# The first routing group computed inside the attention drain, in a transformer block with a mixture of experts

## The reference, cut to what matters

```
x = x + attn_a(layernorm(x))
x = x + ffn(layernorm(x))
x = x + attn_b(layernorm(x))
x = x + ffn(layernorm(x))

def ffn(flat):                                   # 2048 rows
    logits = flat @ router_w                     # 64 experts
    scores = softmax(logits)
    idx    = top_k(logits + router_bias, 4)
    gate   = scores[idx] / scores[idx].sum()
    routed = sum over the 4 of gate * ((silu(flat@wg[e]) * (flat@wu[e])) @ wd[e])
    shared = (silu(flat @ swg) * (flat @ swu)) @ swd
    return routed + shared
```

## Time and profile before

| what | us |
|---|---|
| median of three runs | 1123.34 (1122.24 to 1132.47) |
| the profiled execution's own time | 1131.23 |
| span from its first to its last instruction | 1129.6 |
| PE busy in it | 892.8 (79%) |
| DVE busy | 709.6 (63%) |
| POOL busy | 495.2 (44%) |
| ACT busy | 460.4 (41%) |
| mean granted clock of PE, as a share of full speed | 0.889 |

### The profile page before, as it was taken

The page is one execution under the profiler, slowest core; times in us unless marked ns, Lnnn a source line. Parts: engine busy times, 40 slices in busy tenths (PEclk is TensorE's granted clock), DMA queues, the critical chain, the costliest instruction groups (busy, mean ns, idle before and its releaser), DMA issues. The chain is left out here.

```text
span 1129.6 us, 23684 instructions
## 1 busy us (share of the span) xinstructions
PE 892.8 (79%) x7450; PEld 674.7 (60%) x7450; DVE 709.6 (63%) x2262; ACT 460.4 (41%) x974; POOL 495.2 (44%) x575
## 2 busy tenths in 40 slices
PE   6986999989898888992755799998999797998000
PEld 5764666658787766881644445547888576786000
DVE  6877888846987333553555789946887543454333
ACT  3643565552110444663334468872111144564000
POOL 3000344331777432325772234428577532331775
PEclk9986899998999899996786799998999899999555
DMA  7483999909995799863496677605824498974443
GB/s 263 91 162 66 188 249 235 277 11 267 236 247 163 233 274 271 260 205 115 131 191 169 112 107 114 90 1 130 202 98 136 154 276 249 272 244 144 126 130 116
DMA packets 159162, 197.86 MB, mean 175 GB/s; under 512 B 17376, under 2 KB 137696, under 8 KB 155872
## 3 DMA queue, kind: packets, MB, share of 16 engines
q1 hardware_dynamic: 105920, 101.96, 40.9%
q0 software_dynamic: 22848, 68.18, 18.9%
q10 hardware_dynamic: 30272, 26.22, 7.9%
HBM read 132.86 MB, written 90.18 MB: 197 GB/s over the span
## 5 line engine op out<-in xcount | busy, mean ns | idle before, releaser
L893 ACT ACTIVATE tmp<-ps 128x256 f32<-128x256 f32 (+1 forms) x344 | 155.7, 478 | 115.3 <-PE ps L846 40.6
L518 POOL DMA_INDIRECT xd<-big,slot x128 | 130.2, 1017 | 71.7 <-issue 37.8
L1013 ACT ACTIVATE tmp<-ps 128x384 f32<-128x384 f32 (+1 forms) x256 | 134.9, 544 | 63.5 <-PE ps L662 37.5
L557 POOL DMA_INDIRECT big<-yd,slot x128 | 125.1, 977 | 42.7 <-issue 26.8
L472 POOL COPY arena<-negmax 24x2048 bf16<-24x2048 bf16 x32 | 60.5, 1892 | 136.1 <-ACT negmax L893 91.0
L1152 DVE SCALAR_TENSOR_TENSOR X<-big,comb,X 128x256 f32<-128x256 f32 x128 | 60.1, 483 | 90.7 <-DMA big<-yd,slot 90.5
L579 PE MATMUL ps<-arena 96*128 96x256 bf16 (+1 forms) x512 | 98.8, 280 | 17.2 <-DVE tmp L1203 6.9
L1545 DVE SCALAR_TENSOR_TENSOR tmp<-tmp,ps 128x128 f32<-128x128 f32 x128 | 36.8, 288 | 107.0 <-ACT tmp L1080 106.5
L659 PE MATMUL ps<-arena 120*128 120x256 bf16 (+1 forms) x512 | 101.3, 265 | 0.6 <-ACT tmp L1013 0.2
L1555 DVE COPY tmp<-ps 128x256 f32<-128x256 f32 x128 | 53.8, 424 | 59.0 <-PE ps L875 40.0
L608 PE MATMUL ps<-xt,weights 128*128 128x256 f32 x256 | 72.8, 447 | 22.8 <-ACT xt L893 22.5
(11 more groups left out here) (185 smaller groups left out, 1834.3 us busy)
## 6 DMA issues: line engine op xcount, KB each, us to landing
big<-xd POOLq DMA_DIRECT2D x128, 256.0 KB, 4.7
arena<-parts SPq DMA_DIRECT2D x192, 128.0 KB, 6.0
xd<-zero SPq DMA_DIRECT2D x8, 2048.0 KB, 14.4
spill<-in_we SPq DMA_DIRECT2D x128, 128.0 KB, 2.8
yd<-tmp POOLq DMA_DIRECT2D x64, 256.0 KB, 3.2
yd<-tmp ACTq DMA_DIRECT2D x64, 256.0 KB, 3.3
arena<-in_we SPq DMA_DIRECT2D x8, 1024.0 KB, 8.6
yd<-zero SPq DMA_DIRECT2D x8, 1024.0 KB, 24.6
```

The lines of the kernel that those rows point to most:

```text
L518: pool.indirect_dma_start(xd[:, :], bass.IndirectOffsetOnAxis(ap=slot[:, i, k:k + 1], axis=0), xn_all[:, i, :], None).then_inc(scattered.s ...
L557: pool.indirect_dma_start(gring[n % GRING], None, yd[:, :], bass.IndirectOffsetOnAxis(ap=slot[:, b * TB + m % TB, m // TB:m // TB + 1], ax ...
L893: return act.activation(dst, src, ACT.Copy)
L1013: act.activation(prob[h % 8][:, 0:n], ps[2 + h % 2][:, 0:n], ACT.Exp).then_inc(exp_ready.sem, 1)
```

## The change

Round 0: `turn_normal(0)`, `turn_normal(1)` and `logits(0)` go into the attention's step s = B (behind heads 0 and 3), with DVE's `pick(0)` behind its `group` of head 4; `ranks(0)` and `place(0)` go to step s = B+1. The turned tiles use other PSUM banks there. Round 1: the two turns go into the projection loop behind batches 4 and 5, `logits(0)` behind the loop, `ranks(0)` behind `shared_in(0, 0)`, and DVE does `pick(0)` and `place(0)` one after the other ahead of its first `shared_gate`. In both rounds `pick` and `place` of the other groups each come one shared batch earlier on DVE, `ranks(3)` moves from step 4 to step 3, `share_tiles` moves ahead of `shared_gate(5)`, and the turns and logits of the next group follow `shared_in(s, 1)`. In round 0 POOL scatters two tiles before it normalises the last batch. `EARLY` equals B, so no shared batch moves. The scratch tiles of the routing lie in `spill` now. The diff, cut:

```diff
         def turn_bank(r, b):
+            return ps[7] if b >= TB else ps[b if r == 0 else 2 + b]
+        def rank_bank(r, g):
+            return ps[6] if g else ps[1 if r == 0 else 4]
 # POOL
-                for b in range(B - 1 if r == 0 else 0, B):
-                    normal_rows(b)
+                if r == 1:
+                    for b in range(B):
+                        normal_rows(b)
...
                 for i in range(NT):
+                    if r == 0 and i == TB:
+                        normal_rows(B - 1)
                     if i % 4 == 0:
                         pool.wait_ge(*slot_ready(r, i // 4 + 1))
 # PE, attention loop
+                        if s == B and h == 0 and r == 0:
+                            pe.wait_ge(*mx_ready(r, B * H))
+                            turn_normal(0)
+                            turn_normal(1)
+                        if s == B and h == 3 and r == 0:
+                            logits(0)
+                        if s == B + 1 and h == 3 and r == 0:
+                            ranks(0)
 # PE, projection loop of round 1
+                        if b in (4, 5):
+                            turn_normal(b - 4)
+                    logits(0)
 # PE, shared_in
+                    if s == 0 and half == 1:
+                        pe.wait_ge(*rank_out(r, 1))
 # PE, routing stage
-                turn_normal(0)
-                turn_normal(1)
-                logits(0)
-                turn_normal(2)
-                turn_normal(3)
-                for s in range(B + 1):
-                    if s < B:
+                for s in range(EARLY + 1):
+                    if s < EARLY:
                         shared_in(s, 0)
+                    if s == 0 and r == 1:
+                        ranks(0)
                     if s >= 1:
                         shared_out(s - 1)
-                    if s in (1, 2):
+                    if s < EARLY:
+                        shared_in(s, 1)
+                    if s in (0, 1, 2):
                         turn_normal(2 * s + 2)
                         turn_normal(2 * s + 3)
-                    if s < B:
-                        shared_in(s, 1)
-                    if s in (0, 1, 2, 4):
-                        ranks(min(s, 3))
-                    if s < 3:
                         logits(s + 1)
+                    if s in (1, 2, 3):
+                        ranks(s)
                     if s == 5:
                         pe.wait_ge(*tef_ready(r, 1))
                         pe.transpose(ps[6][0:1, 3 * P:4 * P], tef, ident[:, :]).then_inc(teT_done.sem, 1)
 # ACT, attention loop and projection loop
+                        if s == B and h in (0, 1) and r == 0:
+                            keep_turned(h)
+                        if b in (5, 6):
+                            keep_turned(b - 5)
 # ACT, routing stage
-                for b in range(4):
-                    keep_turned(b)
                 exponents(0)
-                for s in range(B):
+                for s in range(EARLY):
                     shared_tanh(s, 0)
-                    if s in (1, 2):
+                    if s in (1, 2, 3):
+                        exponents(s)
+                    shared_tanh(s, 1)
+                    if s in (0, 1, 2):
                         keep_turned(2 * s + 2)
                         keep_turned(2 * s + 3)
-                    if s in (1, 2, 4):
-                        exponents(min(s, 3))
-                    shared_tanh(s, 1)
 # DVE, attention loop
+                        if s == B and h == 4 and r == 0:
+                            clear_ranks()
+                            pick(0)
+                        if s == B + 1 and h == 4 and r == 0:
+                            place(0)
 # DVE, routing stage
-                pick(0)
+                if r == 1:
+                    clear_ranks()
+                    pick(0)
+                    place(0)
                 shared_gate(0)
-                place(0)
                 pick(1)
                 shared_gate(1)
-                dve.wait_ge(*rp_ready(r, NT))
                 add_shared(0)
                 place(1)
                 pick(2)
                 shared_gate(2)
                 add_shared(1)
                 place(2)
+                pick(3)
                 shared_gate(3)
                 add_shared(2)
-                pick(3)
+                place(3)
+                name_tiles()
                 shared_gate(4)
                 add_shared(3)
-                place(3)
-                name_tiles()
-                shared_gate(5)
-                add_shared(4)
                 share_tiles()
                 gates(0)
                 gates(1)
-                shared_gate(6)
-                add_shared(5)
+                shared_gate(5)
+                add_shared(4)
                 gates(2)
                 gates(3)
                 gates(4)
```

More of the change, by code:

```diff
@@ L50 @@
 EMPTY = E + 128 * E
+EARLY = B
 class Signal:
@@ L1331, in add_out @@
                     variance(r, b)
-                for s in range(B + 2):
-                    first, second, third = s < B, 1 <= s <= B, s >= 2
-                    for h in range(H):
-                        if first:
-                            if s * H + h >= early_maxima:
-                                maximum(s, h)
-                            if h % 8 == 7:
-                                split_maxima(s, h // 8)
-                        if third and h == 0:
-                            group(s - 2, 2)
-                        if third and h == 4:
-                            group(s - 2, 3)
-                        if second and h in (8, 12):
-                            group(s - 1, h // 4 - 2)
-                        if third and h == 9 and r == 0:
-                            dve.wait_ge(op_done.sem, s - 1)
-                            add_out(s - 1, x_added, ps[7])
@@ L1451, in place @@
                     dve.wait_ge(*slot_ready(r, g + 1))
+                for s in range(B + 2):
+                    first, second, third = s < B, 1 <= s <= B, s >= 2
+                    for h in range(H):
+                        if first:
+                            if s * H + h >= early_maxima:
+                                maximum(s, h)
+                            if h % 8 == 7:
+                                split_maxima(s, h // 8)
+                        if third and h == 0:
+                            group(s - 2, 2)
+                        if third and h == 4:
+                            group(s - 2, 3)
+                        if s == B and h == 4 and r == 0:
[3 more added lines that the diff above has]
+                            place(0)
+                        if second and h in (8, 12):
+                            group(s - 1, h // 4 - 2)
+                        if third and h == 9 and r == 0:
+                            dve.wait_ge(op_done.sem, s - 1)
+                            add_out(s - 1, x_added, ps[7])
+                if r == 1:
+                    dve.wait_ge(bias_added.sem, B)
+                    for b in range(B + 1):
+                        if b < B:
+                            dve.wait_ge(op1_done.sem, b + 1)
+                            xb = X[:, b * TB:b * TB + TB, :]
+                            dve.tensor_tensor(xb, xb, ps[6 + b % 2][:, :].rearrange("p (t d) -> p t d", t=TB), ALU.add).then_inc(x1_added.sem, 1)
+                        if b >= 1:
+                            dve.wait_ge(x1_added.sem, b)
+                            for i in range((b - 1) * TB, b * TB):
+                                dve.bn_stats(stats[:, i, :], X[:, i, :]).then_inc(stat_a.sem, 1)
+                            variance(r, b - 1)
                 def name_tiles():
@@ L1532, in _ @@
                 gates(4)
-                shared_gate(7)
-                add_shared(6)
+                for s in range(6, EARLY):
+                    shared_gate(s)
+                    add_shared(s - 1)
                 gates(5)
@@ L1537, in _ @@
                 gates(7)
-                add_shared(7)
+                add_shared(EARLY - 1)
                 barrier(dve, "dve")
```

158 lines of the change are left out of this document (76 added, 82 removed).

## The result

| kernel | median us | runs | range |
|---|---|---|---|
| before | 1127.9 | 4 | 1122.24 to 1137.21 |
| changed | 1147.68 | 4 | 1142.11 to 1152.7 |

The ratio is 1.0193, with a 95% interval of 1.0143 to 1.0243: the change costs 19.8 us between the medians, 1.9%. The profiled execution of the changed kernel took 1152.7 us (span 1151.1, mean clock 0.884 against 0.889), 21.5 more than the one of before. Each is above its median, by 5.0 and 3.3 us, so the traces tell where the time goes and the medians how much it is.

The account below looks back on a forecast made before the run. POOL's scatter chain and the PE-DVE shared-expert chain were taken to bound the kernel together. Round 0 +2.1, round 1 +9.0 and clock +6 made 17, taken as 16: 1123.3 + 16 = 1139 us, range 1133 to 1146.

Parts of the forecast that it names:

- Scatter chain: POOL's scatters up to the first expert load: 11.6 us earlier in round 0, 4.5 in round 1, if nothing else were late.
- Head start of 6.8 and drain: Round 0, attention's end: the drain grows 2.9 us, yet PE begins `shared_in(0, 0)` at 255.0 instead of 261.79.
- Stall at pick(3): PE at step 3, both rounds: waits for DVE, 4.2 us at `ranks(3)` and 0.9 at `shared_in(4, 0)`, 5.1 together.
- The 1.4 at step 5: PE at `shared_in(5, 0)`: waits 1.4 us for DVE's `place(3)` and `name_tiles`, absorbing clock loss from step 4's stalls.
- Stall at share_tiles: PE at `shared_in(6, 0)`: waits for DVE's `share_tiles`, two gates and half a gate, 6.1 us in round 0, 6.2 in round 1.
- Round 1: Start of round 1's shared experts: PE stalls 3.8 us in `ranks(0)` behind `pick(0)`, then 1.6 behind `place(0)`.
- The clock: Slower PE clock behind five idle stretches of 3.8 us or more, two in round 0, three in round 1: +6 us, between 0 and 14.
- The stalls and moves without the clock: Both rounds' routing up to the experts: +2.1 us in round 0 and +9.0 in round 1, +11.1 in sum.
- The rest of the program: Outside the altered stages nothing else that moves costs time; the expert stages keep their length.
- 11 + 14 = 25: Dearer rival: every PE stall drops the clock, for as long as 7 us; total 1148 us, chance 0.10.
- the faster ones: Rival: the scatter was the bound and PE and DVE had slack, so 11.6 and 4.5 us are kept; 1107 us, chance 0.11.
- It decides at `share_tiles`: Faster rival's test: PE keeps its head start only without waits there and at `pick(3)`; without the `share_tiles` stall, sum near +1.

Follow-up runs that it names:

- e9: The kernel before, unaltered, run and traced once more on another chip; ratio 0.9988 to the kernel before.
- e13: The changed kernel with `share_tiles` and its gates back behind `shared_gate(5)` and `add_shared(4)`; ratio 1.0049 to the kernel before.
- e15: The kernel before with only group 0's move, in both rounds, and the changed POOL order; ratio 0.9879 to the kernel before.
- e16: The kernel before with only `share_tiles`, `gates(0)` and `gates(1)` moved ahead of `shared_gate(5)` and `add_shared(4)`; ratio 1.0141 to the kernel before.

## Why the prediction was right in direction and short in size

I forecast +16 and got +19.8; 1139 lies 8.7 below the median, 4.6 of which is that the kernel before itself measured 1127.9 with a fourth run.

- **Scatter chain:** right in round 0: 257.7, 289.9 and 355 forecast, 258.51, 289.79 and 354.85 found. In round 1, counted from its attention, the first scatter came as forecast (794.4; found 804.96 with the attention's end 10.1 later), but POOL then waited 6.71 for group 1 where I had 3.9, and the first load came 2.7 earlier, not 4.5. It was rightly called useless behind PE's stalls.
- **Head start of 6.8 and drain:** right; PE began at 254.08, 255.0 forecast. The drain cost 3.8 where I had 2.9. In the kernel before, that place ran at the lower clock (rows 3 show 3.62 and 3.63 us for eight products that take 1.99 elsewhere); I read the times but gave nothing for this going away.
- **Stall at pick(3):** I had 4.2 + 0.9 = 5.1; it was 3.34 + 0.32 and 3.13 + 0.46. The 1.4 at step 5 didn't come. DVE took what I gave it (16.2 us from the second half of gate 2, at 297.36, to gate 3 at 313.52, against 16.4); it was PE that came later, through the slow products that begin at 278.73 (3.4 us of clock).
- **Stall at share_tiles:** 6.1 and 6.2 forecast, 6.15 and 6.16 found, with 7.83 idle ahead of it on DVE where I had 9.
- **Round 1:** 3.8 and 1.6 forecast at `ranks(0)`, 3.81 and 1.45 found.
- **The clock: this is the step that failed.** The term of +6 was mis-sized: between the two traces it was 11.2, and 17.4 against e9. I priced five stalls at 1.7 (three) and 0.5 (two) us, 6.1 in all; they cost 3.1, 3.1, 2.1, 1.5 and 2.3, 12.1 in all. The wait of 1.4 at step 5 that was to absorb part of it didn't come. I also left out that the clock falls behind the packed turns at step 1 (278.73 in round 0, 821.24 and 824.79 in round 1), with no stall over 1 us ahead: 6.8 more. And the wait of 2.82, behind which I had read nearly full rate, was followed by 5.29 us for products that take 3.62 (1.5 more). On the other side stand the 9.2 us of lower clock that the kernel before had in its trace. What makes the clock fall behind the packed turns in eight rounds of ten and not in the other two stays open.
- The stalls and moves without the clock: 11.1 forecast; 13.5 found in the drain and the two stages (3.8 + 20.9 - 11.2), 13.8 against e9. This part held, within 3 us.
- The rest of the program, which I had said would keep its length: 1.7 us longer between the stages, 4.9 shorter behind the second. In e9 the last part is as short (232.8 against the changed kernel's 232.4), so this is the spread between executions. By it the sum of the traces, 21.5, came nearer to my 17 than the terms did: that much is luck.

The Trainium skill ("TensorE: Matmul & The Clock Gate", HAM oscillation) has TensorE start slow again behind each of a row of waits for a DMA, and I noted that by it the sum would come near the upper end, 11 + 14 = 25. This case's trace agrees for the waits: all five were followed by slow products, 12.1 us of a possible 14.

The rivals: none of the faster ones came. "It decides at `share_tiles`" was right in kind: with that order alone put back the sum is +5.5 us (e13), and I had "near +1". What no rival had is that group 0's move by itself gains, 13.6 us by the medians and 8 by what the traces can place. My own terms gave it only the head start of 6.8 less the drain, and I had it eaten by the stalls in the same sum, so the change's gain and its orders' losses never stood side by side: -13.6, +16.2 (`share_tiles`), +8.9 (`pick(3)`), +10.2 (turns and round 1's order), together +21.7, which is 1.0193 at 1126.33 us. By the intervals each of the four is known to within 6 to 8 us only. The best version measured is e15, 1109.91 us against 1126.33.

## What to carry to other kernels

When a change bundles a move with new orders, price each order alone: here the move gained 1.2% and three reorderings around it lost 3.1%. An instruction that waits for another engine's last product before a reuse gate (DVE's `share_tiles`, which waits for PE's step 5, ahead of the gate that PE's step 6 needs) puts both engines' idle time in series; place it behind the gate. And count the lower clock behind PE's stalls beside the stalls: in the changed kernel 24.8 us of them were followed by 12.1 of clock, half again; behind e16's two of 6.14 and 6.16 it was 4.2, a third. Before laying a slow stretch to an order, look whether it begins ahead of the order, as most of e16's did, and whether a second trace of the same program has it.

## What the runs showed of the hardware

- The granted clock can fall without a long stall. In e15's round 1 stage it was 1.00, with no stall over 1.70 us until step 8's 2.82; in the changed kernel 0.92, with products of 3.76 us (eight; 1.95 at full clock) behind gaps that are all under 1 us.
- Where it falls differs between executions of one program: from 780 to 788 us, 3.0 us lost, in round 1's stage of the kernel before, and nowhere in that stage in e9.
- The kernel before took 1126 to 1128 us in three comparisons and 1236 to 1242 in three others, each on another chip, 10% apart, with instructions late on all engines in the slower ones, and the ratio of a change of 2% differed between them (1.0193 and 1.0001). What makes them late was not found.
